# Decoder block in float32 on one core: ScalarE copies the transposed keys and queries before the output's high part

## What is computed

```python
x = x + attn(_layernorm(x), wq, wk, wv, wo)                 # 32 heads of 16
q = rmsnorm((ln(x) @ Wq.T)) ; k = rmsnorm(ctx @ Wk.T) ; v = ctx @ Wv.T   # 32 heads of 128, 8 key/value heads
scores = einsum('bhqd,bhkd->bhqk', q, k) / sqrt(128) + mask
out = einsum('bhqk,bhkd->bhqd', softmax(scores), v)
x = x + out @ Wo.T
x = x + ffn(_layernorm(x))
```

## Time and profile before

| | |
|---|---|
| device time, median of 3 | 1908.59 us |
| the profiled execution: its own time | 1905.66 us |
| its span, first to last instruction | 1903.9 us |
| TensorE busy (matmuls) | 1724.8 us, 91% |
| VectorE, ScalarE, GpSimd busy | 48%, 39%, 38% |
| granted TensorE clock, mean | 0.966 |
| cross-attention of the two halves | about 217 to 815 and 1159 to 1757 us of the span |

### The profile page before, as it was taken

One profiled execution on the slowest core, in us unless ns is written; L12 is line 12 of the kernel. 1 busy time (PEld: TensorE's weight loads), 2 busy tenths in 40 slices (PEclk: granted clock), 3 DMA queues, 4 the chain that ended last, 5 costly groups with the idle time before them and its releaser, 6 DMA issues.

```text
span 1903.9 us, 29620 instructions
## 1 busy us (share of the span) xinstructions
PE 1724.8 (91%) x11352; PEld 1395.4 (73%) x11352; DVE 913.8 (48%) x1629; ACT 749.4 (39%) x1332; POOL 724.7 (38%) x539
## 2 busy tenths in 40 slices
PE   3899799999999999989959988999999999999898
PEld 1745677777777777878937556777777777777797
DVE  3178434444444444474451783444444444445654
ACT  2366433444434434431222763343434444344311
POOL 2187333343424433451022872424433434244410
PEclk8889999999999999999958998999999999999999
DMA  4110010110101101110041100101101101011100
GB/s 152 37 39 18 17 40 17 39 39 22 50 17 39 55 17 44 33 46 17 18 143 34 34 7 17 39 17 39 55 17 39 39 21 51 17 44 45 34 23 23
DMA packets 25871, 70.92 MB, mean 37 GB/s; under 512 B 3152, under 2 KB 3152, under 8 KB 25808
## 3 DMA queue, kind: packets, MB, share of 16 engines
q1 hardware_dynamic: 25808, 70.05, 11.9%
HBM read 65.85 MB, written 4.19 MB: 37 GB/s over the span
## 4 chain that ended last, share of the span: by engine, by line
PE 77%; DVE 6%; ACT 5%; POOL 5%; issue 4%; DMA 2%; ACTq 0%; SPq 0%; POOLq 0%; DVEq 0%
PE acc L358 13%; PE acc L360 12%; PE acc L359 12%; PE y L358 8%; PE y L360 8%; PE y L359 8%; PE acc L376 4%; PE sc L553 4%; PE ot L567 4%; PE pt L399 2%; POOL prob L1352 2%; ACT kt L842 1%; POOL prob L1358 1%; DMA kv<-in_ctx 1%; ACT w_hi L713 1%
## 5 line engine op out<-in xcount | busy, mean ns | idle before, releaser
L1339 POOL TENSOR_TENSOR w_lo<-stage,w_hi 128x1024 fp32r<-128x1024 f32 (+1 forms) x116 | 250.8, 2174 | 216.5 <-ACT w_hi L713 216.5
L1352 POOL TENSOR_TENSOR prob<-prob,pmax 128x512 f32<-128x512 f32 x128 | 133.5, 1043 | 446.6 <-DVE pmax L1028 446.4
L358 PE MATMUL y<-w_hi 128*128 128x512 f32 x576 | 232.9, 404 | 0.0
L358 PE MATMUL acc<-w_hi,xn_hi 128*128 128x512 f32 (+1 forms) x576 | 226.7, 394 | 2.9 <-DVE xn_lo L986 2.9
L360 PE MATMUL y<-w_hi,w_lo 128*128 128x512 f32 x576 | 225.7, 392 | 0.0
L359 PE MATMUL y<-w_lo,w_hi 128*128 128x512 f32 x576 | 224.5, 390 | 0.0
L360 PE MATMUL acc<-w_hi,xn_lo 128*128 128x512 f32 (+1 forms) x576 | 219.6, 381 | 0.0
L359 PE MATMUL acc<-w_lo,xn_hi 128*128 128x512 f32 (+1 forms) x576 | 219.2, 381 | 0.0
L1358 POOL TENSOR_TENSOR prob<-prob,prec 128x512 f32<-128x512 f32 x128 | 141.0, 1101 | 107.0 <-DVE prec L1036 107.0
L1022 DVE TENSOR_TENSOR prob<-sc,mask 128x512 f32<-128x512 f32 x64 | 44.3, 692 | 270.4 <-PE sc L553 270.4
L1343 POOL TENSOR_TENSOR qkrs<-qkve,mhalf 128x10 f32<-128x10 f32 x64 | 125.0, 1953 | 119.3 <-DVE qkve L1073 117.7
(11 more groups left out here) (128 smaller groups left out, 3787.7 us busy)
## 6 DMA issues: line engine op xcount, KB each, us to landing
stage<-in_w_cross SPq DMA_DIRECT2D x64, 512.0 KB, 3.6
stage<-in_w_cross SPq DMA_DIRECT2D x32, 256.0 KB, 2.7
stage<-in_w_ffn SPq DMA_DIRECT2D x16, 512.0 KB, 3.5
kv<-in_ctx SPq DMA_DIRECT2D x16, 256.0 KB, 3.8
x<-in_x SPq DMA_DIRECT2D x8, 512.0 KB, 6.6
stage<-in_w_self SPq DMA_DIRECT2D x8, 512.0 KB, 3.9
out_x<-x SPq DMA_DIRECT2D x16, 256.0 KB, 2.0
stage<-in_w_self SPq DMA_DIRECT2D x4, 256.0 KB, 6.6
```

The source lines that it names most:

```text
L358: nc.tensor.matmul(target, l_hi, r_hi, start=first, stop=False)
L1339: nc.gpsimd.tensor_tensor(low, stage[:, place.slot(n), 0:width], high.bitcast(F32), ALU.subtract).then_inc(w_lo_done, 1)
L1352: nc.gpsimd.tensor_tensor(pr, pr, spread(pmax[:, buffer, :], 8, SEQ), ALU.subtract).then_inc(s_sub.sem, 1)
```

## The change

The instructions are the same, and their number is the same. Only their order in the lists of ScalarE and GpSimd is another; TensorE's, VectorE's and SyncE's lists are untouched. In every slot the high part of the output goes to the end of ScalarE's slot, behind the transposed keys and queries, and in slot 3 also behind the splits of pieces 10 and 11. In slot 1 pieces 6 and 7 are split ahead of the exponential, piece 8 ahead of the copy of the transposed probabilities, and piece 9 right behind that copy. GpSimd splits piece 6 before it subtracts the maximum and piece 7 before it multiplies. In the hand-written last turn, chunk 3's transposed keys and queries are copied ahead of chunk 2's high part.

```diff
@@ ScalarE, slot @@
                 if front:
                     keys_and_values(place, k + 2)
+                if next_group and k == 1:
+                    act.wait_ge(acc_rdy.sem, at(acc_rdy, 6 * 3 + C_KV + 1))
+                    split_piece(place, 6)
+                    split_piece(place, 7)
                 if mid:
                     exps(at, k + 1, (k + 1) % PRING)
                 if front:
                     queries(place, k + 2, 0)
-                if next_group and k == 1:
-                    act.wait_ge(acc_rdy.sem, at(acc_rdy, 6 * 3 + C_KV + 1))
-                    split_piece(place, 6)
-                    split_piece(place, 7)
-                if front:
                     queries(place, k + 2, 1)
-                if mid:
-                    evacuate_probs(at, k + 1, (k + 1) % 2)
                 if next_group and k == 1:
                     act.wait_ge(acc_rdy.sem, at(acc_rdy, 6 * 3 + C_Q + 2))
                     split_piece(place, 8)
                 if mid:
-                    outputs_hi(at, k + 1)
+                    evacuate_probs(at, k + 1, (k + 1) % 2)
                 if next_group and k == 1:
                     split_piece(place, 9)
                 if front:
@@
                 if next_group and k == 3:
                     out_weights(place, 10)
                     out_weights(place, 11)
+                if mid:
+                    outputs_hi(at, k + 1)
@@ ScalarE, last turn by hand @@
                 split_piece(place, 1)
+                transposed_chunk(turn.at, 3)
                 outputs_hi(turn.at, 2)
                 split_piece(place, 2)
-                transposed_chunk(turn.at, 3)
                 norm_hi(0)
```

## The result

The changed kernel takes 1924.18 us (median of 4, 1923.78 to 1924.53) against 1908.66 us for the kernel before (median of 4): the ratio is 1.0082, with a 95% interval of 1.0067 to 1.0096. It is slower by 15.5 us, where 48 us less were forecast.

The account below looks back on a forecast made before the run. TensorE, busy 91% of the span, bounds the kernel; its 60.1 us of waits for ScalarE's copy of transposed keys were targeted. 44 × 0.56 + 14 × 1.50 + 2 × 1.4 = 48.4 us gave 1860 us, range 1848 to 1874.

Parts of the forecast that it names:

- The mechanism of the gain: Cross-attention slots: with the high part moved, L842 starts when KT is done, so bank 1 is released earlier for QT1.
- an ordinary slot: Term for 44 cross-attention slots: next keys and values start 1.55 us behind KT instead of 2.11, gaining 0.56 us each.
- slot 1: Term for 14 slots: next keys and values come 1.55 us behind KT instead of 3.05, gaining 1.50 us each.
- the hand-written place: Term for 2 places in the hand-written turn: scores come about 2.39 us behind KT instead of 3.81, gaining 1.4 us each.
- The covers that I named: Claim that moved output parts, splits and loads stay hidden, with slack such as 6.8 us before the output product.
- the late softmax: Rival, chance 0.08: GpSimd's splits delay the softmax in slots 0 and 1, giving about 1888 us.
- the piece not landed: Rival, chance 0.04: in slot 3 ScalarE waits for piece 11's transfer with the high part queued behind; slower, 1959 at 12 us.
- The whole idle time: Rival, chance 0.06: all of TensorE's 60.1 us waiting for the transposed keys' copy goes, giving 1848.5 us.
- What the moved work costs: Step checking each moved instruction's cover in the slots; it claimed nothing is added and took no cost into the sum.
- third rival: Chance 0.03: VectorE's scaling, which releases KT, holds TensorE instead, about 1908 us; dismissed as its 1.1 us slack stays.
- the rule that I weighed: GpSimd contends with VectorE instructions having two SBUF inputs; so the low part, with one, would not stretch piece 10's split.

Follow-up runs that it names:

- e1: The changed kernel with ScalarE splitting piece 8 behind the copy of the transposed probabilities again, its old place; 1859.52 us, ratio 0.9745 to the kernel before.
- e2: The changed kernel with one added wait: in slot 1 GpSimd waits for the end of VectorE's scaling before splitting piece 8; 1858.32 us, ratio 0.9735.
- e3: The kernel before with only the output's high part moved, all weight pieces at their old places; 1858.81 us, ratio 0.9744.
- e6: The changed kernel with GpSimd in slot 1 waiting for VectorE's scaling only before piece 9, piece 8 staying ahead; 1874.32 us, ratio 0.9820.
- e5: The changed kernel with 12 more matmuls, changing no result, ahead of the transposed keys in slot 1, where TensorE otherwise stands; 1907.51 us, ratio 0.9991.
- e7: The changed kernel with GpSimd splitting pieces 8 and 9 in two instructions of 512 columns each; 1874.37 us, ratio 0.9822.

## Why the prediction was wrong

**What held.** The mechanism of the gain and its size. L842 starts behind KT; QT1 and the next keys and values follow as worked out; ordinary slots take 18.37 us where 18.35 was forecast; slot 1 is as short where it is not disturbed (e1: 18.37). Term by term: 0.54 us for an ordinary slot (0.56 forecast), 1.50 for slot 1 (1.50), and 1.44 for the hand-written place (1.4), where the scores come 2.38 us behind KT in place of 3.82. The sum, 1860 us, is what e1 (1859.5), e2 (1858.3) and e3 (1858.8) measure. The covers that I named held too: no TensorE wait for the low part of the output inside the loop, none for the probabilities there, and no ScalarE or GpSimd wait for a weight piece's transfer. That refutes the late softmax and the piece not landed. The whole idle time is refuted by the 18.37 us: a slot is 0.54 us shorter, not 0.76.

**The step that failed** is in "What the moved work costs": it has no term for GpSimd's split of piece 8, so this stood at nothing without a reason, and it cost 67 us (44 of waiting and 23 of the slower matmuls behind it). At slot 1 it says "GpSimd is done with both splits before the reciprocal roots are asked for, as now". That was said of pieces 6 and 7, and it held (658.84 against 662.75). For piece 8 I followed ScalarE's instruction to its new place and not the GpSimd instruction that it releases. ScalarE's part of piece 8 moved ahead of the probabilities' copy. So GpSimd's part was ready when the roots ended, at the very moment at which the roots also release VectorE's scaling. Both start from one event, GpSimd won by 0.07 us, and VectorE stood for 2.16 and 2.14 us. The slack of KT behind the scaling, 1.1 us, was in the prediction (third rival); 4.3 less 1.1 gives the 3.2 us that TensorE waits.

**The row that showed it.** I read the split's 3.23 us as GpSimd made slower beside L1083, by 0.86 us, and asked only what that would cost the GpSimd side. The row fits a wait better: the split ends at 659.22, and 2.38 us before that, the time of a split alone (e6), is 656.84, about the end of L1083 (657.00). An engine that stands 0.86 us for the rest of a 1.22 us instruction would make the other stand for up to the 2.4 us of a split if the order were turned. In the kernel before the two were close: L1083 started at 655.78 and the split at 655.99.

The turned order was even in the trace of the kernel before, in the feed-forward part, which neither of my readings covered. There a split begins first, and VectorE's subtraction of two SBUF tensors, at most 0.70 us beside nothing, takes 2.42:

```profile
844.39 2.35 POOL L1339 TENSOR_TENSOR w_lo<-stage,w_hi 128x1024 fp32r<-128x1024 f32 x1 [2.55 <-ACT w_hi L713]
```
```profile
844.86 2.42 DVE L986 TENSOR_TENSOR w_lo<-qb,w_hi 128x512 fp32r<-128x512 f32 x1 [0.91 <-ACT w_hi L915]
```

So the price of the turned order could have been read before the change was run. The Trainium skill states the rule outright (SBUF — State Buffer, section "SBUF: two separate sides"): whichever of the two starts first has the shared pair for the whole instruction and the other fully blocks. The traces agree, with 2.60 us for 0.43 in e6. By that page the rule that I weighed was only half of it: I cited which instructions contend and not who pays.

**The second loss**, the clock, was in no rival. I took a wait of TensorE to cost its own length. Here each 3.2 us cost another 1.64 us, which e5 gives back. The kernel before had such a place in slot -1: after its 3.02 us wait, KT lasts 0.69 us and not 0.44, and the slot behind takes 20.42 us where an ordinary one took 18.91.

**The third rival** named the right instruction (the scaling that releases KT) and dismissed it because "it starts from TensorE's own query product". That is true of its start, and its start was on time. It was its duration that changed.

What stays open: why the parts outside the cross-attention's slots differ from profile to profile (748 us in the changed kernel, 753 before, 755 in e5, from the span less the two stretches from slot -1's KT to the last; 2.9 us of the first difference are the hand-written place). It decides nothing above.

## What to carry to other kernels

When a step moves, follow what it releases on the next engine, and ask what else that event or moment releases: two engines that share something and start together are a race that an order of instructions decides. A duration that is longer in one row than in other rows of the same line and shape can be a wait that the profile does not list (here it was); find the other party and ask what it would pay if it came second. Where the order matters, fix it with a wait (e2, 1858 us); shortening the blocking instruction brought back less (e7, 1874 us). And price a TensorE wait of about 3 us above its length.

## What the runs showed of the hardware

- GpSimd's subtraction of two SBUF tensors and VectorE's product of two SBUF tensors exclude each other for about a whole instruction, in either order: 0.43 becomes 2.60 us behind a split of 2.40 (e6), 1.51 behind one of 1.30 (e7); the split becomes 3.23 behind L1083. With several queued on both sides they alternate (e7).
- Two tensors in SBUF are not the only case. VectorE's layer norm step L1116 (a TENSOR_SCALAR, with one SBUF tensor and two single columns as inputs) takes 0.54 to 0.55 us in 6 of its 16 instructions and 1.26 in the 10 that start 0.07 us behind a GpSimd subtraction of 1.04 us. From VectorE's records of the kernel before (shortest, median and longest, in ns):

```profile
L1116 DVE TENSOR_SCALAR xn<-x,mv,rstd x16: 537/1256/1262, 140.4 to 1155.8; 128x512 f32<-128x512 f32 x16
```
- VectorE's subtraction and addition with one input in PSUM are not held. Beside the splits of 10 and 11 in the changed kernel, the low part and the mask keep their times:

```profile
633.98 4.75 POOL L1338 TENSOR_TENSOR w_lo<-stage,w_hi 128x1024 fp32r<-128x1024 f32 x2 [6.01 <-ACT w_hi L713]
```
```profile
635.79 1.23 DVE L985 TENSOR_TENSOR w_lo<-ot,w_hi 128x1024 fp32r<-128x1024 f32 x1 [5.39 <-ACT w_hi L853]
636.93 0.68 DVE L1021 TENSOR_TENSOR prob<-sc,mask 128x512 f32<-128x512 f32 x1
```

- The standing time is counted as busy: VectorE's busy time rose from 913.8 to 971.3 us with the same 1629 instructions, about the 14 × 4.3 = 60 us of standing.
- A TensorE wait of 3.2 us is followed by a stretch at a granted clock of 0.50; one of 1.06 us (e6) is not.
